# Second expert layer of a gated attention block: from tiles listed on the chip to one fixed region and unit per expert

## The chip, the cores and the metric

One core of one Trainium2 chip. The metric is the device time of one execution in microseconds (us), median of three runs; lower is better. The engines are named as in the profile: PE (TensorE), PEld (its weight loads), DVE (VectorE), ACT (ScalarE), POOL (GpSimd) and SP (SyncE, here only a DMA queue).

## What is computed

Four layers run over x, 4 x 256 = 1024 tokens of 256 floats: an attention map that keeps the top 30% of each row, a first feed-forward layer with 4 fixed experts, a softmax attention, and a second feed-forward layer with 64 experts, of which each token picks 8. Only the last is changed:

```
x = x + tanh(g_ffn[1]) * ffn(layernorm(x))

probs = softmax(xn @ gate_w)                      # 1024 x 64
top_vals, top_idx = top_k(probs, 8);  top_vals /= sum(top_vals)
rw = zeros(1024, 64).at[token, top_idx].set(top_vals)
g = einsum('th,ehi->tei', xn, w_gate)             # 64 experts, 256 -> 96
u = einsum('th,ehi->tei', xn, w_up)
h = silu(g) * u * rw[:, :, None]
out = einsum('tei,eih->th', h, w_down)            # 96 -> 256, summed over experts
```

1024 tokens make 8192 picks. On the inputs of this case the reference sends between 93 and 169 tokens to an expert: 93 tiles of 128 slots when each expert's rows are cut into tiles of 128, and no expert with more than 192. All values are float32.

## The kernel before

Every engine has a program of its own, written out in order; engines wait for each other through semaphores, and an instruction that waits holds back all behind it on its engine. SP issues the loads of weights, POOL the indirect DMAs.

**Up to the router** (0 to 139 us) the layers run in halves or quarters `b` of 256 tokens. On DVE `choose_experts(b)` (L1041 to L1047) takes the top 8 of the logits and writes the 0/1 matrix `chosen`. For b = 0, 1 it stands ahead of `add_layer0(2)` (L1000), with which the layers of the last two quarters go on.

**Lists** (139 to 150 us). PE counts the picks per expert (L652) and ranks each one (L657, L659); DVE works out how many tiles of 128 slots each expert needs and which expert each tile belongs to; the count goes into registers (`over_tiles`), so the loop over tiles has a length that is known only on the chip, in quads of four lanes (`Tile`).

**The loop over tiles** (150 to 472 us), 96 of them. `slot_lists` (PE L673, from `one_hot` and `cols` that DVE's `prepare` builds) finds the tokens of a tile and their weights; `copy_lists` on ACT turns them into row numbers. POOL's `gather` (L472) fetches 128 rows of the normed tokens into `x_slots`, five tiles ahead. PE transposes them (L681), multiplies with gate and up weights (L691) and with the down weights (L698); ACT weighs the result into `y_slots` (L902), and POOL's `scatter` (L481) adds the 128 rows to a sum in DRAM (`expert_sums`, two copies of it, used in turn, since two additions to a row must not overlap). POOL's order is scatter(j-1), gather(j+5). PE's order in a slot is

```
gate_up1(tile)
down1(tile.before())
slot_lists(tile.later(AHEAD))
transpose_slots(tile.later(2))
```

**End** (472 to 484 us): SP reads both sums back, DVE adds them, SP stores.

Of the kernel before, what the change touches and what calls it, by code (L numbers as in the profile page):

```python
# [14 lines left out]
P = 128  # L15
# [9 lines left out]
LANES = 4  # L25
PARTS = 3
W_SCALE = 4096.0
N_COLS = 1 + PARTS
FIRST_QUADS = 2
LAST_QUADS = 2  # L30
AHEAD = 5
N_SUMS = 2


def gated_layers_kernel(nc, x, ctx_in, mask_ss, mask_bs, g_xattn, g_ffn, wq0, wk0, gamma_raw, gate_up, down,
                        wq1, bq1, wk1, bk1, router_w, w_gate, w_up, w_down, out):
# [9 lines left out]
    NE, _, I1 = w_gate.shape  # L46
# [10 lines left out]
    MIN_QUADS = T * TOP_K_EXPERTS // P // LANES  # L57
    MAX_QUADS = P // LANES
    MAX_COUNT_TILES = T // P

    xn_dram = nc.dram_tensor("normed_rows", [T + P, D], F32, kind="Internal").ap()
    sums_dram = [nc.dram_tensor(f"expert_sums{n}", [T + P, D], F32, kind="Internal").ap() for n in range(N_SUMS)]

    with ExitStack() as stack:
# [13 lines left out]
        proj_t = sb("proj_t", [C, 4, T])  # L78
# [48 lines left out]
        zeros = sb("zeros", [P, 2 * BANK])  # L127
# [5 lines left out]
        rank = sb("rank", [P, NT, NE])  # L133
        w_rest = sb("w_rest", [P, PARTS - 1, NT, NE])
        w_parts = sb("w_parts", [P, NT, NE, PARTS], F16)
        n_tiles = sb("n_tiles", [P, NE])
        n_tiles_i = sb("n_tiles_i", [P, 2, NE], I32)
        tiles_end = sb("tiles_end", [P, NE])
        list_scratch = sb("list_scratch", [P, 2, NE])
        row_id = sb("row_id", [P, 1])  # L140
        empty_row = sb("empty_row", [P, 1])
        token_id = sb("token_id", [P, NT])
        slot_id = sb("slot_id", [P, P, NT], F16)
        tile_of = sb("tile_of", [P, 4])
        tile_diag = sb("tile_diag", [P, 2, P])
        first_rank = sb("first_rank", [P, P])
        expert_of = sb("expert_of", [1, P], I32)
        n_quads = sb("n_quads", [1, 4], I32)
        local = sb("local", [P, 2, NT], F16)
        one_hot = sb("one_hot", [P, 2, P, NT], F16)  # L150
        cols = sb("cols", [P, 2, NT, N_COLS], F16)
        w_seen = sb("w_seen", [P, 2, PARTS])
        slot_w = sb("slot_w", [P, P])
        gather_at = sb("gather_at", [P, LANES], U32)
        scatter_at = sb("scatter_at", [P, LANES], U32)
        x_slots = sb("x_slots", [P, LANES, D])
        x_slots_t = sb("x_slots_t", [P, 2, KC, P])
        wg = sb("wg", [P, LANES, KC, I1])
        wu = sb("wu", [P, LANES, KC, I1])
        wd = sb("wd", [I1, LANES, D])  # L160
        silu1 = sb("silu1", [I1, 2, P])
        h1_t = sb("h1_t", [I1, 2, P])
        y_slots = sb("y_slots", [P, LANES, D])
# [19 lines left out]
        part_ready, rest_w_ready = sem("part_ready"), sem("rest_w_ready")  # L183
        zeros_ready, consts_ready = sem("zeros_ready"), sem("consts_ready")
        scratch_zeroed, x3_ready, x3_stored, xn_stored = sem("scratch_zeroed"), sem("x3_ready"), sem("x3_stored"), sem("xn_stored")
        chosen_ready, diag_ready, lists_ready = sem("chosen_ready"), sem("diag_ready"), sem("lists_ready")
        cols_ready, list_filled, list_copied = sem("cols_ready"), sem("list_filled"), sem("list_copied")
        gathered = [sem(f"gathered{n}") for n in range(LANES)]
        w_landed = [sem(f"w_landed{n}") for n in range(LANES)]
        scattered = [sem(f"scattered{n}") for n in range(N_SUMS)]  # L190
        xt_filled, xt_copied, gu_filled = sem("xt_filled"), sem("xt_copied"), sem("gu_filled")
        silu1_ready, h_ready, y_filled, y_ready = sem("silu1_ready"), sem("h_ready"), sem("y_filled"), sem("y_ready")
        local_ready, rows_kept = sem("local_ready"), sem("rows_kept")
        gathers_begun, scatters_begun, weighing = sem("gathers_begun"), sem("scatters_begun"), sem("weighing")
        sums_loaded = [sem(f"sums_loaded{c}") for c in range(B)]
# [55 lines left out]
        add_down_fill(2 * NE0 - 1)  # L251
        F_YT[2], F_YT[3] = add_fill("yt", "dve"), add_fill("yt", "dve")
        for b in (2, 3):
            F_XNT2[b] = add_fill("xnt2", "act")
            F_LOGIT[b] = add_fill("logit", "act")
        F_COUNT = add_fill("count", "dve")
        F_RANK = add_fill("rank", "dve")
        F_TILES = add_fill("tiles", "dve")
# [38 lines left out]
        class Tile:  # L297


            def __init__(self, quad, lane):  # L300
                self.quad, self.lane = quad, lane
                self.j = quad * LANES + lane
                self.two = lane % 2

            def later(self, n):
                return Tile(self.quad + (self.lane + n) // LANES, (self.lane + n) % LANES)

            def sum(self):

                return self.lane % N_SUMS, self.quad * (LANES // N_SUMS) + self.lane // N_SUMS  # L310

            def before(self):
                return self.later(-1)

        def over_tiles(eng, slot):

            eng.wait_ge(lists_ready, 1)
            inner_quads = eng.value_load(n_quads[0:1, 0:1], min_val=MIN_QUADS - FIRST_QUADS - LAST_QUADS,  # L320
                                         max_val=MAX_QUADS - FIRST_QUADS - LAST_QUADS)
            for quad in range(FIRST_QUADS):
                for lane in range(LANES):
                    slot(Tile(quad, lane), None)
            with eng.Fori(FIRST_QUADS, inner_quads + FIRST_QUADS) as quad:
                for lane in range(LANES):
                    slot(Tile(quad, lane), None)
            for n in range(LAST_QUADS * LANES):
                slot(Tile(inner_quads + FIRST_QUADS, 0).later(n), LAST_QUADS * LANES - 1 - n)
            return Tile(inner_quads + FIRST_QUADS + LAST_QUADS - 1, LANES - 1)  # L330

        def follows(left, n):

            return left is None or left >= n

        def first(tile):
            return isinstance(tile.j, int) and tile.j == 0
# [4 lines left out]
        def _(sp):  # L342
# [17 lines left out]
            sp.wait_ge(zeros_ready, 1)  # L360
            z_rows = zeros[:, 0:2 * BANK].rearrange("p (r d) -> p r d", d=D)
            for rows in sums_dram[1:]:
                for n in range(NT // 4):
                    sp.dma_start(rows[n * 4 * P:(n + 1) * 4 * P, :].rearrange("(p r) d -> p r d", p=P), z_rows).then_inc(scratch_zeroed, 16)
            for rows in (*sums_dram, xn_dram):
                sp.dma_start(rows[T:T + P, :], zeros[:, 0:D]).then_inc(scratch_zeroed, 16)
            sp.wait_ge(x3_ready, NT)
            sp.dma_start(sums_dram[0][0:T, :].rearrange("(t p) d -> p t d", p=P), x3[:]).then_inc(x3_stored, 16)
            sp.wait_ge(xn_ready, 2 * NT)
            sp.dma_start(xn_dram[0:T, :].rearrange("(t p) d -> p t d", p=P), xn[:]).then_inc(xn_stored, 16)  # L370
# [824 lines left out]
```

## Time and profile before

| | |
|---|---|
| time, median of 3 runs | 486.61 us (486.55 to 488.47) |
| span of the profiled execution | 484.2 us |
| PE busy | 333.1 us (69%) |
| DVE busy | 241.1 us (50%) |
| ACT busy | 206.3 us (43%) |
| POOL busy | 292.6 us (60%) |
| granted TensorE clock, mean over the span | 0.843 of 2.4 GHz |
| moved by the DMA engines | 65.19 MB |

The only time of the profiled execution is its span; the median lies 2.4 us above it, and that is taken as what lies around the span. A matmul's duration in the page includes its passage through the array, which overlaps the next one; what it costs in a row of matmuls is read from the start of one group to the start of the next.

### The profile page before, as it was taken

What the parts mean: (1) busy time and instruction counts of PE and PEld (TensorE: products, weight loads), DVE (VectorE), ACT (ScalarE), POOL (GpSimd) and SP (SyncE); (2) the same over time, 40 slices, a digit from 0 to 9 for tenths busy, and PEclk for the clock granted to TensorE, in tenths of its full rate; (3) what the DMA queues carried; (4) which work ended last, traced back from release to release, by engine and by line L of the source; (5) the groups of instructions that cost most, each with busy time, mean ns of one, the idle gap of its engine ahead of it and who ended that gap; (6) DMA issues with size and microseconds to landing.
All of it is one profiled execution on the core that took longest, in us unless ns stands there. A gap on an engine that the chain in (4) does not pass through costs nothing.

```text
span 484.2 us, 10739 instructions
## 1 busy us (share of the span) xinstructions
PE 333.1 (69%) x2285; PEld 276.9 (57%) x2286; DVE 241.1 (50%) x971; ACT 206.3 (43%) x812; POOL 292.6 (60%) x255
## 2 busy tenths in 40 slices
PE   5894481574343977689787988869667888878630
PEld 2432480474232866578676777758656777767520
DVE  0999999866885434433333434344434433433102
ACT  2254433174652544453444445344445444444320
POOL 3820130232124578788787878787887878888760
PEclk9999996688555899987879779797999887879985
DMA  4900000000055588777787888887878877888858
GB/s 119 373 24 0 2 1 0 2 1 0 1 167 143 123 182 174 166 160 157 165 184 172 169 174 176 170 167 180 172 155 158 165 167 173 181 171 168 178 73 271
DMA packets 68771, 65.19 MB, mean 135 GB/s; under 512 B 10640, under 2 KB 64400, under 8 KB 68752
## 3 DMA queue, kind: packets, MB, share of 16 engines
q0 software_dynamic: 18432, 25.18, 32.1%
q1 hardware_dynamic: 50320, 39.80, 27.7%
q8 instruction: 6, 0.10, 0.1%
q14 instruction: 13, 0.11, 0.1%
HBM read 47.78 MB, written 17.17 MB: 134 GB/s over the span
## 4 chain that ended last, share of the span: by engine, by line
DMA 24%; PE 20%; DVE 20%; issue 19%; POOL 7%; ACT 5%; POOLq 1%; DVEq 1%; SPq 1%; another core or an unknown queue 1%; ACTq 0%
DMA expert_sums<-y_slots,scatter_at 17%; PE psum L691 6%; DMA x_slots<-normed_rows,gather_at 5%; POOL expert_sums L481 5%; DVE work L970 4%; DVE top L966 4%; PE psum L681 3%; PE psum L673 2%; PE psum L698 2%; DVE stats L941 2%; POOL x_slots L472 2%; PE psum L517 2%; PE psum L511 2%; PE psum L607 1%; DMA adj<-expert_sums 1%
## 5 line engine op out<-in xcount | busy, mean ns | idle before, releaser
L481 POOL DMA_INDIRECT expert_sums<-y_slots,scatter_at x96 | 159.1, 1657 | 33.5 <-issue 27.9
L1152 DVE TENSOR_TENSOR h_t<-silu,psum 96x128 f32<-96x128 f32 x96 | 27.2, 283 | 193.1 <-ACT silu L888 81.7
L472 POOL DMA_INDIRECT x_slots<-normed_rows,gather_at x96 | 96.5, 1005 | 38.8 <-issue 18.7
L681 PE MATMUL psum<-ident,x_slots 128*128 128x128 f32 x192 | 51.6, 355 | 50.5 <-DMA x_slots<-normed_rows,gather_at 44.5
L673 PEld LDWEIGHTS psum<-cols,one_hot 128*128 128x128 f16 x768 | 61.9, 165 | 27.2 <-issue 18.1
L691 PE MATMUL psum<-x_slots_t,wg 128*96 128x128 f32 x384 | 69.5, 311 | 8.8 <-issue 6.1
L698 PE MATMUL psum<-wd,h_t 96*128 96x256 f32 x192 | 67.1, 435 | 4.2 <-issue 3.4
L691 PE MATMUL psum<-x_slots_t,wu 128*96 128x128 f32 x384 | 66.4, 302 | 0.0
L1146 DVE TENSOR_TENSOR one_hot<-slot_id,local 128x1024 f16<-128x1024 f16 x96 | 65.7, 685 | 0.0
L673 PE MATMUL psum<-cols,one_hot 128*128 128x4 f16 x768 | 59.6, 199 | 6.7 <-DVE one_hot L1146 5.4
L691 PEld LDWEIGHTS psum<-x_slots_t,wg 128*96 128x96 f32 x384 | 55.7, 190 | 14.2 <-issue 10.7
L681 PEld LDWEIGHTS psum<-ident,x_slots 128*128 128x128 f32 x192 | 31.0, 210 | 55.9 <-DMA x_slots<-normed_rows,gather_at 42.4
L895 ACT COPY scatter_at<-gather_at 128x1 uint32<-128x1 uint32 x96 | 18.1, 189 | 103.2 <-DMA expert_sums<-y_slots,scatter_at 101.0
L691 PEld LDWEIGHTS psum<-x_slots_t,wu 128*96 128x96 f32 x384 | 55.5, 187 | 0.0
L902 ACT ACTIVATE y_slots<-psum,slot_w 128x256 f32<-128x256 f32 x96 | 45.6, 475 | 22.5 <-PE psum L698 8.8
L427 POOL TENSOR_TENSOR rstd<-var_eps,minus_half 128x2 f32<-128x2 f32 (+1 forms) x13 | 10.5, 804 | 61.2 <-DVE var_eps L947 61.2
L888 ACT ACTIVATE silu<-psum 96x128 f32<-96x128 f32 x96 | 26.7, 278 | 26.0 <-PE psum L691 10.8
L883 ACT COPY x_slots_t<-psum 128x256 f32<-128x256 f32 x96 | 35.5, 370 | 4.6 <-PE psum L681 3.8
L698 PEld LDWEIGHTS psum<-wd,h_t 96*128 96x128 f32 x192 | 33.6, 219 | 6.0 <-issue 4.6
L966 DVE MAX8 top<-work 128x8 f32<-128x256 f32 x72 | 26.6, 409 | 0.0
L564 PE MATMUL psum<-ident,xn 128*128 128x128 f32 x32 | 7.6, 385 | 26.5 <-ACT xn L769 26.5
L873 ACT ACTIVATE w_seen<-psum 128x3 f32<-128x3 f32 x96 | 16.6, 173 | 21.2 <-PE psum L673 11.4
(146 smaller groups left out, 436.5 us busy)
## 6 DMA issues: line engine op xcount, KB each, us to landing
wg<-in_L_ffn_w_gate SPq DMA_DIRECT2D x96, 96.0 KB
wu<-in_L_ffn_w_up SPq DMA_DIRECT2D x96, 96.0 KB
wd<-in_L_ffn_w_down SPq DMA_DIRECT2D x96, 96.0 KB
gu_w<-in_L_ffn_gate_up_proj SPq DMA_DIRECT2D x4, 512.0 KB, 8.1
x_slots<-normed_rows,gather_at POOLq DMA_INDIRECT x96
expert_sums<-y_slots,scatter_at POOLq DMA_INDIRECT x96
xs<-in_x SPq DMA_DIRECT2D x1, 1024.0 KB, 5.6
down_w<-in_L_ffn_down_proj SPq DMA_DIRECT2D x4, 256.0 KB, 8.1
```

What stands on the lines that cost most here:

```text
L472: pool.indirect_dma_start(x_slots[:, tile.lane, :], None, xn_dram, bass.IndirectOffsetOnAxis(ap=gather_at[:, tile.lane:tile.lane + 1], axi ...
L481: pool.indirect_dma_start(sums_dram[n], bass.IndirectOffsetOnAxis(ap=scatter_at[:, tile.lane:tile.lane + 1], axis=0), y_slots[:, tile.lane ...
L673: last = pe.matmul(psum[:, tile.two, 0:N_COLS], one_hot[:, tile.two, :, t], cols[:, tile.two, t, :], start=t == 0, stop=t == NT - 1)
L681: last = pe.transpose(psum[:, 2 + tile.two, k * P:(k + 1) * P], x_slots[:, tile.lane, :].rearrange("p (n k) -> p k n", k=KC)[:, k, :], ide ...
L691: last = pe.matmul(psum[0:I1, 4 + tile.two, part * P:(part + 1) * P], w[:, tile.lane, k, :], x_slots_t[:, tile.two, k, :], start=k == 0, s ...
L698: pe.matmul(psum[:, 6 + tile.two, 0:D], h1_t[:, tile.two, :], wd[:, tile.lane, :], start=True, stop=True).then_inc(y_filled, 1)
L883: act.copy(x_slots_t[:, tile.two].rearrange("p k n -> p (k n)"), psum[:, 2 + tile.two, 0:D]).then_inc(xt_copied, 1)
L888: act.activation(silu1[:, tile.two], psum[0:I1, 4 + tile.two, 0:P], ACT.Silu).then_inc(silu1_ready, 1)
L902: act.activation(y_slots[:, tile.lane, :], psum[:, 6 + tile.two, 0:D], ACT.Copy, scale=slot_w[:, bass.ds(tile.j, 1)]).then_inc(y_ready, 1)
L966: dve.max(top8[:, t, r], (work if r else sim)[:, t]).then_inc(top8_ready, 1)
L1146: dve.tensor_tensor(one_hot[:, two], slot_id[:], local[:, two:two + 1].to_broadcast([P, P, NT]), ALU.is_equal).then_inc(cols_ready, 1)
L1152: dve.tensor_tensor(h1_t[:, tile.two], silu1[:, tile.two], psum[0:I1, 4 + tile.two, P:2 * P], ALU.mult).then_inc(h_ready, 1)
```

## The change

The lists, the gathers and the additions in DRAM go. Each expert owns a region of 1024 rows in `rows_dram`, and the first 192 rows of each are filled with empty rows at the start. As soon as a quarter is routed, each token's normed row (256 floats) is pushed into the region of each of its 8 experts, with 64 more words behind it (`ROW` = 320) that say to which row of `picks_dram` the result goes: one row per token and pick. A unit is then one expert and its first 192 slots, as 96 partitions by 2 rows. It loads them with one plain DMA, and puts its result out with two indirect DMAs of 96 rows, to the rows that the loaded words name; empty slots name none. There are 63 units in a straight line (experts 1 to 63), and a loop for expert 0 and for what lies past 192 in a region (here one turn in all). The weights and the sum over the 8 picks come at the end: per 128 tokens, 8 matmuls with a diagonal matrix of the weights. Gate and up weights of an expert lie together in one array and come with one DMA, into a ring of 8 (`W_RING`); rows, results and picks have rings of 4.

```diff
-            for rows in sums_dram[1:]:
-                for n in range(NT // 4):
-                    sp.dma_start(rows[...], z_rows)
-            sp.dma_start(sums_dram[0][0:T, :].rearrange("(t p) d -> p t d", p=P), x3[:])
-            sp.dma_start(xn_dram[0:T, :].rearrange("(t p) d -> p t d", p=P), xn[:])
+            by_expert = rows_dram[0:NE * T].rearrange("(e r) d -> e (r d)", e=NE)
+            sp.dma_start(by_expert[:, 0:CAP * ROW].rearrange("e (p n) -> p e n", p=SLOTS),
+                         empty_rows[0:SLOTS]...to_broadcast([SLOTS, NE, SUBS * ROW])).then_inc(rows_cleared, 16)
+            def load_weights(e):
+                n = e % W_RING
+                need(sp, y_filled, e - W_RING + 1)
+                sp.dma_start(wgu[:, n].rearrange("p k n -> p (k n)"), w_gate_up[(e + 1) % NE]).then_inc(w_landed[n], 16)
+                sp.dma_start(wd[:, n], w_down[(e + 1) % NE]).then_inc(w_landed[n], 16)
+            def load_rows(e):
+                n = e % X_RING
+                need(sp, scattered[n], 16 * SUBS * (e // X_RING))
+                sp.dma_start(x_slots[0:SLOTS, n].rearrange("p i d -> p (i d)"),
+                             by_expert[e + 1, 0:CAP * ROW].rearrange("(p n) -> p n", p=SLOTS)).then_inc(x_landed[n], 16)
+            for b in range(B):
+                sp.wait_ge(placed[b], 16 * HB * TOP_K_EXPERTS)
+            for e in range(X_RING):
+                load_rows(e)
+            for e in range(UNITS):
+                if e + W_RING <= UNITS:
+                    load_weights(e + W_RING)
+                if e + X_RING < UNITS:
+                    load_rows(e + X_RING)
...
+            picks_f = picks_dram.rearrange("(t p k) d -> t p (k d)", p=P, k=TOP_K_EXPERTS)
+            for t in range(NT):
+                need(sp, picks_summed, t - K_RING + 1)
+                sp.dma_start(picks[t % K_RING], picks_f[t]).then_inc(picks_landed[t % K_RING], 16)
...
-            def gather(tile):
-                pool.indirect_dma_start(x_slots[:, tile.lane, :], None, xn_dram, ...)
-            def scatter(tile):
-                pool.wait_ge(y_ready, tile.j + 1)
-                need(pool, scattered[n], earlier * 16)
-                pool.indirect_dma_start(sums_dram[n], ..., compute_op=ALU.add).then_inc(scattered[n], 16)
+                    # place_rows: once for each of 8 tiles of tokens and 8 picks
+                    pool.indirect_dma_start(rows_dram, bass.IndirectOffsetOnAxis(ap=place_at[:, t, k:k + 1], axis=0),
+                                            x_rows[:, t, :], None).then_inc(placed[b], 16)
+            def scatter(e):
+                n = e % Y_RING
+                pool.wait_ge(y_ready, e + 1)
+                for i in range(SUBS):
+                    pool.indirect_dma_start(picks_dram, bass.IndirectOffsetOnAxis(ap=x_slots[0:SLOTS, n, i, D + e + 1:D + e + 2].bitcast(U32), axis=0),
+                                            y_slots[0:SLOTS, n, i, :], None, bounds_check=T * TOP_K_EXPERTS - 1, oob_is_err=False).then_inc(scattered[n], 16)
...
+            transpose_slots(0)
+            transpose_slots(1)
+            for e in range(UNITS):
+                gate_up1(e)
+                if e:
+                    down1(e - 1)
+                if e + 2 < UNITS:
+                    transpose_slots(e + 2)
...
+            for t in range(NT):
+                pe.wait_ge(diag_ready, t + 1)
+                pe.wait_ge(picks_landed[t % K_RING], 16 * (t // K_RING + 1))
+                for k in range(TOP_K_EXPERTS):
+                    last = pe.matmul(psum[:, t, 0:D], diag[:, t % 2, k, :], picks[t % K_RING][:, k * D:(k + 1) * D], ...)
...
             choose_experts(0)
             choose_experts(1)
+            place_rows(0)
+            place_rows(1)
             for b in (2, 3):
                 add_layer0(b)
```

**PE, inside the run over the experts.** One tile before: find its slots, transpose, gate, up, down. `x_slots_t` is the transposed input, `wg`, `wu`, `wd` the weights.

```order
L673 MATMUL psum<-cols,one_hot 128x4 x8
L681 MATMUL psum<-ident,x_slots 128x128 x2
L691 MATMUL psum<-x_slots_t,wg 96x128 x2
L691 MATMUL psum<-x_slots_t,wu 96x128 x2
L698 MATMUL psum<-wd,h_t 128x256
```

The first units now. The new buffers lie in older tensors: rows, their transpose and h are parts of `gu_w`, the down weights of `proj_t`.

```order
L699 MATMUL psum<-ident,gu_w 128x96 x8
L710 MATMUL psum<-gu_w,wgu 96x192 x4
L699 MATMUL psum<-ident,gu_w 128x96 x4
L710 MATMUL psum<-gu_w,wgu 96x192 x4
L719 MATMUL psum<-proj_t,gu_w 96x256 x2
L699 MATMUL psum<-ident,gu_w 128x96 x4
```

The matmuls that made the lists are gone. Per unit there are 4 transposes of 96 columns, 4 products of 192 columns and 2 of 256; the transposes of unit e+2 stand behind down of unit e-1, as before.

**POOL, from the last `h_t` of the first expert layer on.** Before: statistics (`rstd`, `shift`), two subtractions, five gathers, then scatter and gather in turn.

```order
L427 TENSOR_TENSOR rstd<-var_eps,minus_half 128x2
L429 TENSOR_TENSOR shift<-neg_mean,rstd 128x2
L462 TENSOR_TENSOR w_rest<-rw,w_parts 128x512
L462 TENSOR_TENSOR w_rest<-w_rest,w_parts 128x512
L472 DMA x_slots<-normed_rows,gather_at 128x256 x5
```

Now, down to the turns of the last loop (`gu_w` holds the row numbers, `down_w` the results):

```order
L473 DMA expert_rows<-x_rows,place_at 65728x320 x2
L434 TENSOR_TENSOR rstd<-var_eps,minus_half 128x2
L436 TENSOR_TENSOR shift<-neg_mean,rstd 128x2
L473 DMA expert_rows<-x_rows,place_at 65728x320 x2
...
L473 DMA expert_rows<-x_rows,place_at 65728x320 x51
L314 TENSOR_LOAD over_total
L494 DMA token_picks<-down_w,gu_w 8192x256 x126
```

64 pushes stand ahead of everything that the units scatter, with the statistics of the last two quarters among the first 13 of them.

**SP, where the units are fed.** Before, weights alone (the rows came through POOL); now weights and rows in turn, `gu_w<-expert_rows` being the rows of a unit.

```order
L381 DMA wg<-in_L_ffn_w_gate 128x192
L382 DMA wu<-in_L_ffn_w_up 128x192
L383 DMA wd<-in_L_ffn_w_down 96x256
```

```order
L314 TENSOR_LOAD over_total
L356 DMA gu_w<-expert_rows 96x640 x4
L350 DMA wgu<-in_L_ffn_w_gate_up 128x384
L351 DMA proj_t<-in_L_ffn_w_down 96x256
L356 DMA gu_w<-expert_rows 96x640
```

Four units' rows are asked for at once; from then on one unit's at a time, each behind a wait of its own (`need(sp, scattered[n], ...)`).

## Rows read from the trace of the kernel before

**Rows 1.** The page's costliest groups: busy us, mean ns, idle before and its end.
```profile
L481 POOL DMA_INDIRECT expert_sums<-y_slots,scatter_at x96 | 159.1, 1657 | 33.5 <-issue 27.9
L472 POOL DMA_INDIRECT x_slots<-normed_rows,gather_at x96 | 96.5, 1005 | 38.8 <-issue 18.7
...
L902 ACT ACTIVATE y_slots<-psum,slot_w 128x256 f32<-128x256 f32 x96 | 45.6, 475 | 22.5 <-PE psum L698 8.8
```

**Rows 2.** Timeline of POOL in the loop: start us, us, what, idle before.
```profile
168.71 0.99 POOL L472 DMA_INDIRECT x_slots<-normed_rows,gather_at  x1 [0.30 <-ACT gather_at L877]
170.00 1.69 POOL L481 DMA_INDIRECT expert_sums<-y_slots,scatter_at  x1 [0.30 <-issue]
```

**Rows 3.** Windows: us, busy PE, PEld, DVE, ACT, POOL, granted clock, DMA share, GB/s.
```profile
20.00:24.00 4.00, 3.28 (x9) 2.50 (x8) 4.00 (x19) 1.18 (x2) 3.62 (x6) 1.00 1.07 389
220.00:300.00 80.00, 68.06 (x497) 59.05 (x496) 30.30 (x120) 37.00 (x174) 64.56 (x50) 0.81 0.80 168
```

**Rows 4.** Timeline of PE, one tile without a gap at clock 1.00.
```profile
333.81 0.47 PE L681 MATMUL psum<-ident,x_slots 128*128 128x128 f32 x2
334.11 0.60 PE L691 MATMUL psum<-x_slots_t,wg 128*96 128x128 f32 x4
334.55 0.60 PE L691 MATMUL psum<-x_slots_t,wu 128*96 128x128 f32 x4
334.99 0.60 PE L698 MATMUL psum<-wd,h_t 96*128 96x256 f32 x2
335.42 0.60 PE L673 MATMUL psum<-cols,one_hot 128*128 128x4 f16 x8
```

**Rows 5.** Timeline of DVE where the pushes will be prepared: start us, us.
```profile
113.40 0.23 DVE L1047 TENSOR_SCALAR chosen<-logits_left 128x128 bf16<-128x128 f32 x1
```

**Rows 6.** DMA issues: KB each, median us from issue to landing.
```profile
xs<-in_x SPq DMA_DIRECT2D x1, 1024.0 KB, 5.6
...
out<-xs SPq DMA_DIRECT2D x4, 256.0 KB, 2.2
ctx_rows<-in_ctx SPq DMA_DIRECT2D x1, 256.0 KB, 3.0
```

**Rows 7.** Timeline of PE, one tile at half the granted clock.
```profile
432.51 0.70 PE L681 MATMUL psum<-ident,x_slots 128*128 128x128 f32 x2 [0.42 <-DMA x_slots<-normed_rows,gather_at]
433.00 1.06 PE L691 MATMUL psum<-x_slots_t,wg 128*96 128x128 f32 x4
433.86 1.06 PE L691 MATMUL psum<-x_slots_t,wu 128*96 128x128 f32 x4
434.71 1.06 PE L698 MATMUL psum<-wd,h_t 96*128 96x256 f32 x2
435.56 0.63 PE L673 MATMUL psum<-cols,one_hot 128*128 128x4 f16 x8
```

**Rows 8.** Chain that ended last, around the first result: start, us, what.
```profile
162.25 0.48 ACT y_slots L902
...
163.56 1.30 POOL expert_sums L481
```

**Rows 9.** The same chain: a gather from its issue to its landing.
```profile
372.00 3.34 DMA x_slots<-normed_rows,gather_at
```

**Rows 10.** Timeline at the end: a scatter and the first thing that waits for it.
```profile
468.08 1.55 POOL L481 DMA_INDIRECT expert_sums<-y_slots,scatter_at  x1 [0.91 <-DMA expert_sums<-y_slots,scatter_at]
...
471.94 1.94 SPq L389 DMA_DIRECT2D base<-expert_sums  x4
```

**Rows 11.** Landing times of all DMAs that touch the sums in DRAM.
```profile
DMA to landing us min/median/max: 2.8/4.9/7.8
```

**Rows 12.** Windows of 1 us around a stop of PE (columns as in rows 3).
```profile
230.00:231.00 1.00, 0.07 (x2) 0.00 (x0) 0.00 (x0) 1.00 (x7) 0.75 (x1) 1.00 0.63 161
...
232.00:233.00 1.00, 0.77 (x4) 0.58 (x5) 0.40 (x2) 0.00 (x0) 0.69 (x2) 0.88 0.82 106
...
236.00:237.00 1.00, 1.00 (x10) 1.00 (x9) 0.97 (x5) 0.87 (x5) 1.00 (x1) 0.92 0.62 180
```

More of the change, by code:

```diff
@@ L295, in need, with load_over, load_over_expert @@
                 eng.wait_ge(semaphore, n)
[L297 to L337, printed above, removed]
+        def load_over(eng):
+            eng.wait_ge(over_ready, 1)
+            return eng.value_load(over_total[0:1, 0:1], min_val=1, max_val=MAX_OVER)
+        def load_over_expert(eng, j):
+            return eng.value_load(over_expert[0:1, bass.ds(j, 1)], min_val=0, max_val=NE - 1)
+        SCATTERED = [16 * SUBS * len(range(n, UNITS, Y_RING)) for n in range(Y_RING)]
         block = stack.enter_context(nc.Block())
@@ L653, in _ @@
             last.then_inc(bank_filled, 1)
-            begin(F_RANK)
-            rank_ps = bank(F_RANK).rearrange("p (t e) -> p t e", t=NT)
-            pe.matmul(rank_ps, before[:], chosen[:], start=True, stop=False)
-            for t in range(NT - 1):
-                last = pe.matmul(rank_ps[:, t + 1:NT, :], ones_b[:], chosen[:, t:t + 1, :].to_broadcast([P, NT - 1 - t, NE]),
-                                 start=False, stop=t == NT - 2)
-            last.then_inc(bank_filled, 1)
-            begin(F_TILES)
@@ L690, in gate_up1 @@
+            def gate_up1(e):
+                n = e % W_RING
+                pe.wait_ge(xt_copied, e + 1)
+                pe.wait_ge(w_landed[n], 32 * (e // W_RING + 1))
+                need(pe, h_ready, e - 1)
+                for part in range(2):
                     for k in range(KC):
-                        last = pe.matmul(psum[0:I1, 4 + tile.two, part * P:(part + 1) * P], w[:, tile.lane, k, :],
-                                         x_slots_t[:, tile.two, k, :], start=k == 0, stop=k == KC - 1)
+                        last = pe.matmul(psum[0:I1, 2 + e % 2, part * CAP:(part + 1) * CAP], wgu[:, n, k, part * I1:(part + 1) * I1],
+                                         x_slots_t[:, e % 2, k, :], start=k == 0, stop=k == KC - 1)
@@ L710, in _, with down1 @@
[L710 to L715 removed]
+            def down1(e):
+                n = e % W_RING
+                pe.wait_ge(h_ready, e + 1)
+                need(pe, y_ready, e - 1)
+                for i in range(SUBS):
+                    last = pe.matmul(psum[0:SLOTS, 4 + e % 2, i * D:(i + 1) * D], h1_t[:, e % 2, i * SLOTS:(i + 1) * SLOTS], wd[:, n, :],
+                                     start=True, stop=True)
+                last.then_inc(y_filled, 1)
@@ L905, in slot @@
-            def slot(tile, left):
-                silu_gate(tile)
-                if not first(tile):
-                    weigh(tile.before())
-                if follows(left, 1):
-                    keep_rows(tile.later(1))
-                if follows(left, AHEAD):
-                    copy_lists(tile.later(AHEAD))
-                if follows(left, 2):
-                    copy_slots_t(tile.later(2))
-            for n in range(LANES):
-                copy_lists(Tile(0, n))
-            keep_rows(Tile(0, 0))
```

626 lines of the change are left out of this document (349 added, 277 removed).

## The prediction, made before the changed kernel had run

> **What bounds it now.** I read the page's groups first, then POOL's timeline, windows over the loop and PE's timeline. In the loop POOL issues a gather of 0.99 us and a scatter with addition of about 1.6 us per tile, each with 0.30 us before it that waits for nothing [rows 1, 2]: 3.2 us. The first scatter starts at 163.56 [rows 8] and the 95th at 468.08 [rows 10]: 3.24 us a tile. So POOL bounds the loop. PE is busy for 68 of 80 us, at a mean clock of 0.81, and the DMA engines for 0.80 of the time at 168 GB/s [rows 3]. At full clock a tile costs PE only 0.30 us for 2 transposes, 0.44 for gate, 0.44 for up and 0.43 for down, plus the lists [rows 4], about 2.1 us. The rest of PE's time is slack and half clock.
>
> **Up to the first unit.** The second quarter's `chosen` is ready at 113.6 us [rows 5]. `place_rows(0)` on DVE adds nine small instructions; with scans and products of 128x64 and the waits between them I take 2.5 us, so the first push starts at about 116.2. The two calls put back the last two quarters' layers by about 4 us, which is covered: they only have to be routed before POOL reaches their pushes, 42 us later. There are 64 pushes of 128 rows. A push is not in the trace. It lies between the gather (0.99, the same 128 rows, no addition) and the scatter with addition (1.6), both plus 0.30 [rows 1, 2]; I take the gather, since the addition is what a push lacks. 64 x 1.29 = 83 us, and the four statistics that stand among them 5 us: the last push starts to land at 204 and has landed at 206.5. Until then PE does nothing; no unit may start before all pushes have landed. The clearing of the regions moves 64 x 192 x 1280 bytes = 15.7 MB, 40 us at the 389 GB/s of the loads [rows 3], from about 30 to 70 us, behind nothing that is waited for until 116; the other waits it replaces (zeroed sums, x3 stored) were short. The rows of the first unit, 96 x 2560 bytes = 246 KB, land 3.0 us after issue, as 256 KB did [rows 6]. First transposes: 209.5 us.
>
> **A unit on PE.** At full clock, by columns from rows 4: 4 transposes of 96 instead of 2 of 128 columns, 0.30 x 1.5 = 0.45; gate and up with 192 columns, 0.88 x 1.5 = 1.32; down twice 256 columns (two halves of the slots), 0.87. Together 2.64 us. At half clock, in the same way from 0.49, 0.86 + 0.85 and 0.85 [rows 7]: 0.74, 2.57 and 1.70, together 5.0 us. POOL has two scatters of 96 rows, 2 x 1.29 = 2.6 us at most by the gather. The DMA engines move 295 KB of weights, 246 KB of rows and at most 197 KB of results, 4.4 us at 168 GB/s, less in larger pieces. If these were all, a unit would cost 2.7 to 4.4 us.
>
> **The loop through the ring of rows.** They are not all. The rows of unit e+4 go into the buffer of unit e, and that buffer also holds the row numbers with which the results of unit e are scattered. So SP may load e+4 only when both scatters of e have landed, and PE, in order, comes from the transposes of e+2 to down of e and from there needs e+4 two units later. Two units last as long as this loop: transposes, gate, up and down of one unit, W; then ACT's copy of 512 columns, 0.7 (256 columns took 0.475 [rows 1], so between 0.5 and 0.95); POOL starts 0.5 later (0.82 after the first result [rows 8], 0.3 at best [rows 2]); the second scatter starts 1.29 after the first; it lands 3.5 after its start (a gather 3.34 [rows 9], a scatter with addition 3.86 at the quiet end [rows 10]); SP and PE react, 0.15 in all; the rows land 3.0 after issue [rows 6]. Without W that is 9.1 us. Its bounds are 7.5 (0.5, 0.3, 1.05, 3.34, 0.1, 2.2 by the 256 KB stores [rows 6]) and 12.7 (0.95, 0.8, 1.9, the median landing 4.9 under load [rows 11], 0.15, 4.0 as an estimate for rows beside other traffic).
>
> The four buffers are filled together at the start, so units come in pairs: two bursts, then a stop of 9.1 - W, 4 to 6 us. What such a stop does to the clock is seen at 230 us: PE stood for 1.8 us, the clock fell to 1.2 GHz just after it restarted and stayed there until 236 [rows 12]. So the first burst of each pair runs partly at half clock; I take W = 4.2 between 2.64 and 5.0. Two units: 4.2 + 9.1 = 13.3 us. The first two units take 9.7 us at half clock until down of unit 0 is done (three transposes of units, a copy, two times gate and up, one down), 219.2 us. 62 units later, 31 x 13.3 = 412, down of unit 62 ends at 631.
>
> On that loop a page bears too. The Trainium skill, DMA: Bandwidth & Descriptors, section Anatomy of one DMA, gives each transfer a fixed cost of about 2 us, most of it the receipt of the write, however small the transfer. By its fit the scatter would land after 2.2 us and the rows after 2.6, the loop be 1.7 us shorter and the end 53 us earlier; the row of the gather, 3.34 us in place, stands against it. The page TensorE: Matmul & The Clock Gate, section HAM oscillation, says that a wait for a DMA between bursts returns PE to half rate each time; by that W would be 5.0 and the end 25 us later. Row and rule agree on the direction.
>
> **The end.** The one turn of the loop starts when down of unit 62 is out: 0.74 + 0.6 + 2.57 + 0.4 + 0.35 + 1.70 = 6.4 us at half clock, then copy, two scatters and landing, 6.0: 643.5. Then 8 loads of 1 MB; the first lands after 5 us (5.6 behind other loads [rows 6]), the rest come every 3 us. PE sums with 64 products of 256 columns at two passes each, 128 x 0.215 [rows 4] = 27.5 us and 3.4 more for a cold start: 679.5. Addition, store of 128 KB (2.2 [rows 6]) and end, 3 us: a span of 682.5. The profiled execution before has a span of 484.2 and the median is 2.4 above it, so **685 us**, 41% slower.
>
> **Rivals.** *The ring does not bind*: scatters and loads land so fast that PE or POOL set the pace, 2.7 us a unit. Then 209.5 + 9.7 + 62 x 2.7 = 387, +12.4 +5 +27.5 +3 = 435, and 437 us: faster. It needs the loop of two units below (487 - 685)/31 + 13.3 = 6.9 us to beat 486.6 at all, so 4.2 us for what I put at 9.1; the gather's landing and the load's alone are 6.3. For it speaks only that three of the four steps have not been seen in this form. 6%. *The clock stays up*: W = 2.64, 31 x 1.56 = 48 us less, 637 us; for it speaks that the clock still stood at 1.00 in the window in which PE rested, against it that less than 2 us of rest then brought it down, for over 3 us [rows 12]. 22%. *A plain scatter costs as much as one with addition*: pushes 64 x 0.6 = 38 us more, the second scatter 0.6 later and landing 0.4 later, 31 us more: 754 us. 13%. *Clearing is slow*: writes of 2560 bytes to 64 places at a quarter of the rate would end at 190 and put all pushes back by 74 us, 759 us; stores of 1 MB before the loop land about as fast as loads. 4%. *The change does less than it says*, the ring being emptied in another order, would show as units that do not come in pairs; same sum. The forecast itself, 650 to 720 us: 52%, and 3% for longer still.
>
> **Numbers.** Likeliest 685, its own range 650 to 720. Range 600 to 765: below lies the rival that is faster and part of the clock's, above the longest landing times. Such a kernel is measured to about 0.5%. Faster 0.06, within 0.5% 0.01, slower 0.93.
>
> **What would show it.** In the profile after: pushes on POOL from 116 us, 1.3 us apart, to 204; PE idle from about 150 to 209; in the run of the units PE busy well under 70%, with units in pairs 13 us apart and its longest idle before the transposes of L699, released by the DMA of the rows, which SP issued as soon as the second scatter of four units before had landed; a clock between the two levels; the sum at the end 28 to 31 us of PE. A gap between pairs of less than 7 us would make the prediction wrong, as would a push of over 1.9 us, or PE idle behind ACT or DVE instead of the rows.

## The result, and the profile after

670.4 us (median of 4 runs, 667.9 to 671.7) against 486.6: **1.377 times the time before, 95% interval 1.372 to 1.383**. The profiled execution has a span of 666.1 us at a mean granted clock of 0.75. Where some runs of a kernel lie more than 1.5% above its fastest one, a comparison goes by the fast ones alone, and the text gives the others beside them.

The page's groups that set the time (busy us, mean ns, idle before and what ended it), and its DMA issues (KB, us to landing):

```profile
L494 POOL DMA_INDIRECT token_picks<-down_w,gu_w x126 | 115.6, 918 | 305.6 <-ACT down_w L928 251.0
L699 PE MATMUL psum<-ident,gu_w 96*128 96x96 f32 x252 | 48.4, 338 | 175.8 <-DMA gu_w<-expert_rows 175.8
L710 PE MATMUL psum<-gu_w,wgu 128*96 128x192 f32 x504 | 133.5, 427 | 13.0 <-DVE gu_w L1196 13.0
...
L473 POOL DMA_INDIRECT expert_rows<-x_rows,place_at x64 | 62.4, 974 | 23.8 <-issue 23.8
...
expert_rows<-empty_rows SPq DMA_DIRECT2D x1, 15360.0 KB, 69.1
gu_w<-expert_rows SPq DMA_DIRECT2D x64, 240.0 KB, 2.7
```

POOL, which set the pace of the loop before [rows 1, 2], now waits 251 us for results; PE waits 176 us for rows of the regions. No engine is busy throughout. The window over the units (columns as in rows 3) says the same: PE busy 221 of 385 us, the DMA engines a third of the time, against 0.80 before [rows 3].

```profile
215.00:600.00 385.00, 221.09 (x947) 182.81 (x948) 59.03 (x182) 53.05 (x117) 106.46 (x116) 0.76 0.34 100
```

One turn of the loop, from the timeline of PE, ACT, SP and POOL (start us, us, what, idle before and its end):

```profile
351.26 0.90 PE L699 MATMUL psum<-ident,gu_w 96*128 96x96 f32 x4 [5.14 <-DMA gu_w<-expert_rows]
351.95 2.77 PE L710 MATMUL psum<-gu_w,wgu 128*96 128x192 f32 x8
...
354.51 1.91 PE L719 MATMUL psum<-proj_t,gu_w 96*96 96x256 f32 x4
...
356.46 0.58 ACT L928 COPY down_w<-psum 96x512 f32<-96x512 f32 x1 [1.38 <-PE psum L719]
...
357.83 0.92 POOL L494 DMA_INDIRECT token_picks<-down_w,gu_w  x1 [8.17 <-ACT down_w L928]
...
359.05 0.92 POOL L494 DMA_INDIRECT token_picks<-down_w,gu_w  x1 [0.30 <-issue]
...
361.37 0.31 SPq L356 DMA_DIRECT2D gu_w<-expert_rows  x1
...
364.29 0.91 PE L699 MATMUL psum<-ident,gu_w 96*128 96x96 f32 x4 [4.83 <-DMA gu_w<-expert_rows]
```

Read it as a chain. Down ends at 356.42; copy; first scatter 357.83; second 1.22 later; SP issues the next rows 2.32 after the second scatter's start; they are used 2.92 later, and PE, which had finished the pair's second unit at 359.5, has stood for 4.83 us. From the end of down to the next transposes: 7.87 us. The part before it, transposes to down, took 5.16, because the granted clock is 0.50, half of full speed, in the first half of this burst and full only in its second unit (windows of 1 us; granted clock third from the end; that the clock is what costs the time is tested below):

```profile
351.00:352.00 1.00, 0.74 (x5) 0.75 (x6) 0.00 (x0) 0.00 (x0) 0.00 (x0) 0.50 0.49 164
...
358.00:359.00 1.00, 1.00 (x7) 0.89 (x6) 0.01 (x1) 0.33 (x1) 0.75 (x1) 1.00 0.52 180
...
365.00:366.00 1.00, 1.00 (x6) 0.89 (x5) 0.56 (x1) 0.00 (x0) 0.00 (x0) 0.50 0.00 0
```

Not every scatter lands that fast. In this trace the first unit of each pair has its next rows issued 2.3 to 2.4 us after the start of its second scatter. The second unit of the pair has them issued 3.3 to 4.1 us after, while the rows and weights of the first unit are on their way:

```profile
348.33 0.31 SPq L356 DMA_DIRECT2D gu_w<-expert_rows  x1
348.68 0.43 SPq L350 DMA_DIRECT2D wgu<-in_L_ffn_w_gate_up  x1
348.75 0.92 POOL L494 DMA_INDIRECT token_picks<-down_w,gu_w  x1 [0.30 <-issue]
...
352.32 0.31 SPq L356 DMA_DIRECT2D gu_w<-expert_rows  x1
```

PE doesn't wait for that one: its transposes at 356.22 follow down without a stop.

The first scatter of unit 0 and that of unit 62 on POOL's timeline give the mean: (620.81 - 228.14) / 31 = 12.67 us for two units.

```profile
228.14 0.94 POOL L494 DMA_INDIRECT token_picks<-down_w,gu_w  x1 [26.46 <-ACT down_w L928]
...
620.81 0.92 POOL L494 DMA_INDIRECT token_picks<-down_w,gu_w  x1 [0.30 <-issue]
```

### The profile page after: what moved, and what is told of

Its sections match the earlier page's. It is cut to its first block, busy times and chain, and to the rows that moved or that the text cites. A ratio compares the mean times of both kernels' runs of the same rounds, so it can differ in the third digit from the quotient of the medians.

```text
span 666.1 us, 5463 instructions
## 1 busy us (share of the span) xinstructions
PE 349.6 (52%) x1546; PEld 280.2 (42%) x1546; DVE 206.4 (31%) x858; ACT 118.1 (18%) x265; POOL 212.5 (32%) x256
## 4 chain that ended last, share of the span: by engine, by line
PE 31%; DMA 25%; DVE 15%; issue 10%; POOL 7%; another core or an unknown queue 5%; ACT 4%; POOLq 0%; SPq 0%; DVEq 0%; ACTq 0%
DMA gu_w<-expert_rows 14%; PE psum L710 12%; DMA token_picks<-down_w,gu_w 10%; PE psum L719 7%; POOL token_picks L494 5%; PE psum L765 4%; PE psum L699 4%; DVE work L990 3%; DVE top L986 3%; ACT down_w L928 3%; POOL expert_rows L473 2%; DVE xn L1108 1%; DVE stats L961 1%; PE psum L531 1%
## 5 line engine op out<-in xcount | busy, mean ns | idle before, releaser
L494 POOL DMA_INDIRECT token_picks<-down_w,gu_w x126 | 115.6, 918 | 305.6 <-ACT down_w L928 251.0
L699 PE MATMUL psum<-ident,gu_w 96*128 96x96 f32 x252 | 48.4, 338 | 175.8 <-DMA gu_w<-expert_rows 175.8
L710 PE MATMUL psum<-gu_w,wgu 128*96 128x192 f32 x504 | 133.5, 427 | 13.0 <-DVE gu_w L1196 13.0
L699 PEld LDWEIGHTS psum<-ident,gu_w 96*128 96x128 f32 x252 | 38.2, 200 | 197.5 <-DMA gu_w<-expert_rows 190.1
L710 PEld LDWEIGHTS psum<-gu_w,wgu 128*96 128x96 f32 x504 | 107.5, 226 | 20.4 <-DVE gu_w L1196 13.3
L1196 DVE COPY gu_w<-psum 128x384 f32<-128x384 f32 x63 | 35.1, 558 | 230.0 <-PE psum L699 229.1
L719 PE MATMUL psum<-proj_t,gu_w 96*96 96x256 f32 x252 | 82.6, 461 | 0.0
L473 POOL DMA_INDIRECT expert_rows<-x_rows,place_at x64 | 62.4, 974 | 23.8 <-issue 23.8
L719 PEld LDWEIGHTS psum<-proj_t,gu_w 96*96 96x96 f32 x252 | 52.6, 209 | 13.1 <-DVE gu_w L1201 0.4
L928 ACT COPY down_w<-psum 96x512 f32<-96x512 f32 x63 | 36.7, 582 | 50.5 <-PE psum L719 41.3
```

Source lines behind the costliest of these rows:

```text
L473: pool.indirect_dma_start(rows_dram, bass.IndirectOffsetOnAxis(ap=place_at[:, t, k:k + 1], axis=0), x_rows[:, t, :], None).then_inc(placed ...
L494: pool.indirect_dma_start(picks_dram, bass.IndirectOffsetOnAxis(ap=x_slots[0:SLOTS, n, i, D + e + 1:D + e + 2].bitcast(U32), axis=0), y_sl ...
L699: last = pe.transpose(psum[:, e % 2, k * CAP + i * SLOTS:k * CAP + (i + 1) * SLOTS], x_slots[0:SLOTS, n, i, k * P:(k + 1) * P], ident[0:SL ...
L710: last = pe.matmul(psum[0:I1, 2 + e % 2, part * CAP:(part + 1) * CAP], wgu[:, n, k, part * I1:(part + 1) * I1], x_slots_t[:, e % 2, k, :], ...
L719: last = pe.matmul(psum[0:SLOTS, 4 + e % 2, i * D:(i + 1) * D], h1_t[:, e % 2, i * SLOTS:(i + 1) * SLOTS], wd[:, n, :], start=True, stop=True)
L928: act.copy(y_slots[0:SLOTS, n].rearrange("p i d -> p (i d)"), psum[0:SLOTS, 4 + e % 2, 0:SUBS * D]).then_inc(y_ready, 1)
```

## The experiments

Pace is always the distance between the first scatters of unit 0 and unit 62 divided by 62, in us a unit.

**Three, five and eight buffers.** Both rings were changed together; the additional buffers lie in tiles that are free by then (`sim`, `adj`, `pen`).

```diff
-X_RING = 4
-Y_RING = 4
+X_RING = 8      # 3, 5
+Y_RING = 8      # 3, 5
```

Three: 

> Rows and results with 3 buffers instead of 4. Theory (the loop through the ring binds): the loop now spans one unit instead of two, so each unit costs W + R, with W the work of a unit on PE (5.0 to 5.2 us at half clock, since PE rests 8 us before each) and R = 7.9 us from down to the next rows as the trace of the changed kernel shows: 13.0 us a unit instead of 6.3, 62 x 13.0 = 806 us of units and a time near 1080 us. Rival 1 (PE at its half clock is the bound, the ring only follows): 5.0 us a unit whatever the ring, time within 20 us of 670. Rival 2 (POOL or the DMA engines are the bound): no change.

Five: 

> The same with 5 buffers. Theory: the loop spans three units, 3P = W + R = 5.2 + 7.9 = 13.1, P = 4.4 us, 62 x 4.4 = 270 us, time near 550 us; units come in threes, 13 us apart. Rivals 1 and 2: no change, or at most down to 5.0 us a unit, 590 us.

Eight: 

> The same with 8 buffers. Theory: the loop spans six units and would allow 2.1 us a unit, less than PE needs (2.64 at full clock), so PE sets the pace at full clock, 2.7 to 3.1 us a unit; 227 + 62 x 2.9 + 50 = 457 us of span, time 450 to 475, below the kernel before (486.6). Rival 1: 5.0 us a unit, 590. Rival 2: POOL at 2 x 1.22 = 2.44 us would show as no rest on POOL; the DMA engines' 0.34 x 6.3 = 2.1 us a unit as a share near 0.9.

Measured: 1038.4 us with three (one run), 529.0 with five (one run), 480.7 with eight (4 runs; ratio to before 0.989, interval 0.985 to 0.994). With n buffers PE can be n - 2 units ahead of the unit whose results it waits for. The pace was 12.18, 6.33, 4.04 us a unit for n = 3, 4, 5; times n - 2 that is **12.2, 12.7 and 12.1 us: the same loop each time**, spread over one, two and three units. With eight it would allow 2.0 us a unit, and something else sets 3.25. So the loop is shown, and without it the kernel is no slower than before. Three and five buffers came within 4% of the times expected for the loop, 1080 and 550; eight did not reach its 450 to 475. With eight buffers PE goes on at 2.5 us a unit and stops for about 3 us once in three to five units. Such a stop on PE's timeline:

```profile
302.82 0.49 PE L707 MATMUL psum<-ident,gu_w 96*128 96x96 f32 x4
...
305.32 0.49 PE L707 MATMUL psum<-ident,sim 96*128 96x96 f32 x4
308.71 2.72 PE L718 MATMUL psum<-gu_w,wgu 128*96 128x192 f32 x8 [2.90 <-issue]
```

**The row numbers kept apart.** The rings keep four buffers; what ties the rows' buffer to the scatter is cut.

```diff
-                need(sp, scattered[n], 16 * SUBS * (e // X_RING))
+                need(sp, targets_kept, e - X_RING + 1)
...
+                dve.tensor_copy(targets[0:SLOTS, e % 8], x_slots[0:SLOTS, e % X_RING, :, D + e + 1:D + e + 2]...).then_inc(targets_kept, 1)
```

> Both rings keep their four buffers. DVE copies the row numbers of each unit into a small tile of eight entries of their own, right behind its copy of the transposed rows, and the scatter reads them there. SP may then load the rows of four units later as soon as that small copy is made, not when the scatter has landed. Theory (the loop through ACT's copy, two scatters and their landing sets 12.57 us per two units, because the row numbers lie in the buffer that the next rows need): the loop is gone at the same number of buffers. What is left per unit is PE's 2.5 us with the stops that the kernel with eight buffers showed, 3.3 us, so 62 units take about 204 us instead of 390 and the end comes at 475 to 490 us. Rival A (four buffers are too few whatever they wait for, since the rows land late under the load of weights and scatters): little gained, 600 to 670 us. Rival B (the four buffers of results become the ring: copy, two scatters, landing before ACT may write the buffer again): four units per about 5 us, which would not bind; if it did, the longest idle would be ACT's before its copy L928, and the time between 485 and 670.

Measured: 496.8 us in the fastest run, and 505.1, 506.2 and 508.9 in the other three; the pace is 3.68 in the profiled run, which is the one of 508.9. The loop is gone with four buffers: it was the row numbers in the buffer, not the number of buffers. But even the fastest run is 7 us above the 475 to 490 expected. In the profiled run PE waited 46.4 of 195 us for rows. SP's timeline shows why they are late: they are issued behind weights that wait for down.

```profile
311.47 0.35 SPq L351 DMA_DIRECT2D wgu<-in_L_ffn_w_gate_up  x1
311.86 0.43 SPq L352 DMA_DIRECT2D proj_t<-in_L_ffn_w_down  x1
312.34 0.42 SPq L357 DMA_DIRECT2D gu_w<-expert_rows  x1
```

**The same with SP's order turned.**

```diff
-                if e + W_RING <= UNITS:
-                    load_weights(e + W_RING)
                 if e + X_RING < UNITS:
                     load_rows(e + X_RING)
+                if e + W_RING <= UNITS:
+                    load_weights(e + W_RING)
```

> Four buffers with the row numbers kept apart, as before, which gave 505 us where 475 to 490 was expected, and units every 3.7 us where eight buffers have 3.28. There SP issues the rows of four units later behind the weights of eight units later, and those wait until PE has made down of the unit: in its trace the rows' issue follows the weights' each time, and PE waits for the rows. Here SP issues the rows first and the weights behind them; nothing else differs. Theory (the place in SP's order costs 0.4 us a unit): 475 to 485 us, at the pace of eight buffers. Rival (rows that land 3 us after an issue that itself waits for DVE's small copy are late anyway): 500 to 510 us.

Measured: 485.0 us (10 runs, 482.1 to 488.1; 0.996, interval 0.992 to 0.999), pace 3.30. The place in SP's queue was worth about 12 us against the fastest run of the old order, and 20 to 24 against the others. Once it is mended, four buffers do nearly as well as eight (480.7).

**The clock held up.**

```diff
                 if e + 2 < UNITS:
+                    for _ in range(0 if e % 2 else 20):
+                        pe.matmul(psum[:, 7, :], ones_b[:], chosen[:]..., start=True, stop=True)
                     transpose_slots(e + 2)
```

> Before the transposes that wait for rows (those of every second unit) PE makes 20 matmuls of 512 columns into a bank that nothing reads, 4.3 us at full clock, so that it rests for about 1 us of the 4.8 that it rested. Nothing else is changed. Theory (the part of the pair that lies in PE, transposes, gate and up, down of one unit, takes 4.7 to 5.2 us because the clock falls after each stop; at full clock it is 2.64): the granted clock is near 1.0 in the units' run, a pair takes 10.5 us instead of 12.57, 31 pairs give back 64 us, and the time is 600 to 620 us. Rival (that part isn't long by the clock, or the clock falls even after a rest of 1 us): 670 us or somewhat more, where the filling work itself runs at half clock and takes 8.6 us, more than the rest that it fills: up to 31 x 3.8 us more, 790 us.

Measured: 608.7 us (4 runs; 1.252, interval 1.244 to 1.259). The window over the loop has the clock at 1.00, and the wait for rows behind the filling work is 1.29 us:

```profile
240.00:400.00 160.00, 141.81 (x759) 94.54 (x772) 26.92 (x60) 27.28 (x60) 55.07 (x60) 1.00 0.42 126
...
339.84 0.55 PE L699 MATMUL psum<-ident,gu_w 96*128 96x96 f32 x4 [1.29 <-DMA gu_w<-expert_rows]
```

A pair takes (560.53 - 232.12) / 31 = 10.59 us, 2.08 less, 64 us in 31 pairs; the forecast of W = 2.64 at full clock plus the measured 7.87 is 10.51. The filling work also put the first scatter back by 4.0 us (232.12 against 228.14), and the time fell by 61.7. So about 62 to 64 of the 184 us lost are the clock's.

**DVE's late weights.** `router_weights(2)`, `(3)` and all `pick_weights` stood ahead of the first unit's copy on DVE; here they go between the units.

```diff
-            router_weights(2)
-            router_weights(3)
-            for b in range(B):
-                pick_weights(b)
...
+                if e in (4, 6):
+                    router_weights(2 + (e - 4) // 2)
+                if 8 <= e < 8 + 2 * NT and e % 2 == 0:
+                    pick_weights_of((e - 8) // 2)
```

> Only the weights per pick and the last two quarters' router weights move on DVE: from ahead of the first unit into the run of the units (where DVE rests). Theory: the first transposed rows wait 13 us for DVE in the trace of the changed kernel; they start about 10 to 13 us earlier, the rest stays: time 657 to 661. Rival: the start of the units is not on the path that sets the end (a later wait absorbs it): 670.

Measured: 654.6 us (4 runs; 1.347, interval 1.341 to 1.353); the first scatter starts at 215.66 instead of 228.14, 12.5 us earlier, and the pace is unchanged (6.32). The two profiled executions differ by 12.2 us, the medians by 15.8, a little more than the 10 to 13 expected; no cause was sought for those last 3 us. In the changed kernel PE had transposed the first rows and then waited 13 us for DVE, whose last weights ended at 219.5:

```profile
206.33 1.73 PE L699 MATMUL psum<-ident,gu_w 96*128 96x96 f32 x8 [13.08 <-DMA gu_w<-expert_rows]
...
220.49 1.02 DVE L1196 COPY gu_w<-psum 128x384 f32<-128x384 f32 x2 [0.95 <-DVE xn L1108]
221.11 2.87 PE L710 MATMUL psum<-gu_w,wgu 128*96 128x192 f32 x8 [13.04 <-DVE gu_w L1196]
```

**Both together.** Eight buffers, and the kept row numbers (in the old order of SP), each with DVE's weights moved.

Eight: 

> Eight buffers in both rings together with DVE's work for the second FFN's weights moved into the units' run. The two gains have been measured apart: eight buffers 480.7 us, the moved work 12.4 us earlier first scatter and 16 us in all. Theory (the start of the units and their pace are separate terms of one sum): 480.7 - 12 to 16, so 465 to 469 us. Rival (DVE's moved work now stands in the way of the copies of a run that has no slack, 2.5 us a unit on PE): 475 to 485 us.

Kept: 

> Four buffers with the row numbers kept apart, together with DVE's work for the second FFN's weights moved into the units' run. If the sum holds, 12 to 16 us under the kernel that only keeps the row numbers apart: 462 to 475 us, and under the kernel before (486.6). If the moved work blocks DVE's copy of the row numbers, on which SP's loads now wait, 475 to 500 us.

Measured: **471.3 us with eight (4 runs; 0.970, interval 0.964 to 0.975): the fastest of all, and faster than the kernel before**; 491.0 with the kept numbers (1.012, interval 1.006 to 1.019), outside the 462 to 475 forecast: the kernel that only keeps the numbers had itself come out above its forecast, and the pace stayed at 3.63. Eight buffers gained 9.4 us of the 12 to 16, between the theory and its rival: the first scatter came 13.2 us earlier, the pace was 3.30 instead of 3.25, which takes 2.8 back.

**What stops the units at 3.3 us.** Three attempts. The copy of the transposed rows on ACT:

```diff
-                dve.tensor_copy(x_slots_t[:, e % 2]..., psum[:, e % 2, 0:KC * CAP]).then_inc(xt_copied, 1)
+                act.copy(x_slots_t[:, e % 2]..., psum[:, e % 2, 0:KC * CAP]).then_inc(xt_copied, 1)
```

> The kernel with eight buffers, and the copy of the transposed rows out of PSUM is made by ACT instead of DVE; nothing else. With eight buffers PE went on at 2.5 us a unit but stood for about 3 us once in four or five units; at such a stop the transposes had ended at 305.8 and DVE began their copy only at 308.1, while POOL issued scatter after scatter. Theory 1 (DVE's copy is held up while POOL issues indirect transfers back to back; the Trainium skill, page SBUF — State Buffer, says that DVE's copies may need the port pair that POOL holds): with the copy on ACT the stops are gone, 62 units take 2.5 to 2.6 us each instead of 3.28, 43 us less: 435 to 445 us. Theory 2 (the hold isn't DVE's port but lies in the signals between all engines, or in the DMA queues, when POOL is at its limit): the stops stay, 475 to 490 us.

Measured: 477.8 us (4 runs; 0.979, interval 0.971 to 0.986), pace 3.28, 19 intervals of more than 4.2 us between units (15 with eight buffers alone). The stops stay and now hold ACT: in the window from 235 to 430 us PE waited 12.4 us for ACT's copy by the profile, and 15.6 for the product with silu, which was still made by DVE. So DVE's copy alone is not the cause; whether DVE's other instruction has a part in it was not tested. The Trainium skill, SBUF — State Buffer, section Who interferes with whom, says that DVE's copies can contend with POOL for a shared pair of ports when they run in a mode that uses two ports; no run here shows that this copy, which reads PSUM, did.

A break on POOL (`pause` is a tile of its own; first 32 columns without the wait, then, as shown, 512 with a wait for the end):

```diff
             for e in range(UNITS):
                 scatter(e)
+                pool.memset(pause[:], 0.0).then_inc(paused, 1)
+                pool.wait_ge(paused, e + 1)
```

32 columns: 

> The kernel with eight buffers, and POOL clears 32 columns of a tile of its own after the two scatters of each unit, which breaks its run of back-to-back scatters (2.44 us a unit, as long as a unit on PE) by some 0.3 to 0.5 us. If the stops come from scatters issued without a break over several units (theories 1 and 2 alike), there are fewer of them and the units come every 2.8 to 2.95 us: 450 to 465 us, faster with more work. If the breaks don't matter, POOL's added work makes no difference while its mean load is 75%, 478 to 485 us; if POOL is what bounds the run through another way, the added 0.4 us a unit shows: 500 to 510 us.

512 columns, on the fastest version: 

> The fastest version so far (eight buffers, and DVE's later weights in the units' run: 471.3 us, units every 3.3 us, most of them 2.44 us apart with one interval of 5.2 us in three or four), and POOL clears 512 columns of a tile of its own after each unit's two scatters and waits until that is done. The earlier try with 32 columns made no break at all: its 0.14 us lay inside the 0.30 us that stands before each scatter anyway, and the units were 2.44 us apart as before. 512 columns take 0.52 us, so that POOL's units are at least 2.85 to 3.1 us apart. Theory 2 (the stops of PE, DVE and ACT come when POOL has issued six to eight scatters without a break): fewer or no intervals of 5 us, units every 2.9 to 3.1 us, 450 to 463 us. Rival (the stops have another cause and come in their own time): the break adds its length to the intervals between stops, units every 3.5 to 3.8 us, 480 to 500 us.

Measured: 482.9 us with 32 columns (10 runs; 0.993, interval 0.989 to 0.996), pace 3.25: no break, so no test. With 512 columns 480.3 us (6 runs; 0.989, interval 0.986 to 0.992), pace 3.49, and **not one interval above 4.2 us**:

```profile
299.44 0.91 POOL L503 DMA_INDIRECT token_picks<-down_w,gu_w  x1 [0.30 <-issue]
300.35 0.54 POOL L508 MEMSET pause<- 128x512 f32 x1
301.69 0.91 POOL L503 DMA_INDIRECT token_picks<-down_w,gu_w  x1 [0.79 <-issue]
302.90 0.91 POOL L503 DMA_INDIRECT token_picks<-down_w,gu_w  x1 [0.30 <-issue]
```

The break was 1.02 us longer than none, where 0.4 to 0.65 was expected; POOL's two scatters and it take 3.46 us, and that is the pace. Time and pace came out at the edge of what the rival in the expectation had, but its reason did not: the break wasn't added to intervals between stops, the stops were gone. So they vanish when POOL issues two scatters every 3.46 us instead of every 2.44. Two readings remain: unbroken issuing causes them, or something caps the mean at about 3.3 us a unit (3.25, 3.25, 3.28, 3.30, 3.30 in five different kernels) and a steady 3.46 never meets it. A break of half that length would tell; it was not tried.

## Why the prediction was right

It forecast 685 us as likeliest, and the likeliest case happened for the reason given: units in pairs, held by the loop through the buffer that also holds the row numbers. That the number is so close is in part luck, since terms that were off had opposite signs. Against the span, 682.5 was forecast and 666.1 measured: the start came 7.7 us later, the loop was 19.3 shorter, the end 5.0 shorter, 16.6 in all (rounded terms).

- **The pushes.** First at 116.2, 64 times 1.29: the first started at 115.93, they were 1.27 us apart and 0.974 long, the last began at 200.72. The gather was the right stand-in for a push. The clearing took 69 us from 16.3 on, where 40 had been forecast from 30 on; it was over by 85.4, before the first push.
- **The first unit: too early by 7.7 us.** Transposes at 206.33 (209.5 forecast), but the first scatter at 228.14, not 219.2 + 1.2. The step that failed is "no unit may start before all pushes have landed", taken as if nothing else could hold the first unit: it left out DVE, which still had the routing weights to do. PE waited 13.04 us behind DVE there. The prediction had named "PE idle behind ACT or DVE" as a sign against it; it came true at this one place, not in the loop. Moving those weights brought the scatter to 215.66, 4.7 us earlier even than forecast.
- **W, forecast 4.2.** The mean pair less 7.87 is 4.8. With the clock held up, 10.59 less 7.87 leaves 2.72, near the 2.64 at full clock. The Trainium skill, TensorE: Matmul & The Clock Gate, section HAM oscillation, by whose rule the prediction had worked out 5.0, holds here: the measured 4.8 is nearer to it than to my 4.2.
- **The rest of the loop, forecast 9.1: 7.87.** Copy 0.6 and POOL 0.8 after it (1.2 forecast); the second scatter 1.22 later (1.29); landing and SP **2.32 against 3.5**; rows 2.92 (3.0 and reaction). The landing is the term that was mis-sized: 3.5 came from a gather's 3.34 in the loop before [rows 9], where the DMA engines were busy for 0.80 of the time, and the scatter that counts here lands while little else moves. Three more turns of the loop show 2.33, 2.32 and 2.36; the second unit of a pair, whose scatters land beside rows and weights, shows 3.3 to 4.1. So direction and traffic were not told apart, and 2.32 is no figure for every plain scatter. For the landing that counts, the fixed cost in the Trainium skill, DMA: Bandwidth & Descriptors, section Anatomy of one DMA, by which I had worked out 2.2 as an estimate, was the better guide, and I had set it aside. That section is about transfers that POOL issues; the rows come through SP, so the 2.6 that I took from it for them (2.92 measured) was not covered. The errors in W and in the rest partly cancel: 13.3 forecast, 12.67 measured.
- **The end.** 50.3 us were forecast from the first scatter of unit 62, 45.3 measured: the unit over and its landing 8.2 instead of 11.3, the first 1 MB landed after 5.0 as forecast, the sum and the last store the rest.
- **The signs.** PE was busy for 57% of the run of the units and the pairs came 12.67 us apart, as forecast. "A gap between pairs of less than 7 us would make the prediction wrong" does not fit the prediction's own stop of 4 to 6 us: PE stood for 4.8 to 6.4 us between pairs. Only measured from down to the next transposes is the gap 7.87.
- **The rivals.** The clock that stays up would have given 637 by my sum; made to stay up, it gave 608.7, since the loop's other part was also shorter. The ring that doesn't bind was put at 437; the three versions in which only the ring was taken away gave 480.7, 485.0 and 496.8 (fastest run), because of a pace of 3.25 to 3.7, which neither PE (2.5) nor POOL (2.44) explains. Had the ring not bound, that number would have been 40 us off or more. Scatters as dear as with addition (0.92 us, not 1.6) and a clearing so slow that it holds the pushes are refuted by the rows above.

## What to carry to other kernels

When a buffer holds both data and the addresses for a later scatter, the load of its next content waits for the scatter's landing, and the loop divided by the units in flight is the pace: work it out with its latencies before counting anybody's busy time. Copying the row numbers aside (two for each partition), or more buffers, took the loop away here. Then look at what is ahead in each queue: rows behind weights on SP cost 12 us or more, and weights ahead of the first copy on DVE 12, though DVE was busy for only 35 of the 99 us before the units and SP does nothing but issue.

## What was not expected of the hardware

- While POOL issued its pushes without a break, DVE was held for long stretches by nothing that the trace shows. PE had made the ranks of the last quarter by 147.0, yet DVE added to them at 159.99; the counts were there at 147.4 and were copied at 178.22. These two waits alone are 29 us, and the weights that followed ended at 219.5, over 11 us after PE had transposed the first rows; that they would otherwise have been in time is argued, not shown. Shorter waits of this kind went on after the last push had begun at 200.72 (2.25 us before 209.08). The cause is open. On PE's timeline:

```profile
146.77 0.24 PE L668 MATMUL psum<-chosen,before 128*128 128x64 bf16 x1
146.82 0.61 PE L684 MATMUL psum<-chosen,ones_b 128*128 128x64 bf16 x8
```

And on DVE's:

```profile
159.99 0.29 DVE L1080 TENSOR_TENSOR place<-psum,first_row 128x128 f32<-128x128 f32 x1 [12.15 <-issue]
...
178.22 0.23 DVE L1152 COPY counts<-psum 128x64 f32<-128x64 f32 x1 [17.02 <-remote]
```

- The stops with eight buffers hold PE, DVE and ACT alike, 14 to 19 times in 62 units, and none came when POOL's scatters were spread by a further 1.02 us in each unit. Open as well.
- A scatter of 96 rows without addition costs POOL 0.92 us, a push of 128 rows 0.97, against 1.66 with addition [rows 1]. One behind the other they have 0.30 before each in which nothing is waited for; a clearing of 0.14 us between them cost nothing (32 columns above).
- In the windows shown and those between them the granted clock stayed at 1.00 through the rest of 4.8 us and fell to 0.50 only after PE had begun again (0.62 in the window from 364, in which it restarted at 364.29, 0.50 in the next).
